# A vision tower whose first attention gets its input by batch: norm of batch 0 and mixed weights inside the embedding, both product layers by batch

## The reference, cut to what matters

```python
shifted = jnp.pad(x, ((0, 0), (1, 0), (0, 0)))[:, :-1]
delta = shifted - x
xr, xw, xk, xv, xa, xg = [x + delta * x_mix[i] for i in range(6)]
r = xr @ W_r
w = DECAY_SCALE * sigmoid(tanh(xw @ A_w) @ B_w + b_w)
k = xk @ W_k
v = xv @ W_v
a = sigmoid(xa @ A_a @ B_a + b_a)
g = sigmoid(xg @ A_g) @ B_g
```

## Time and profile before

| | us |
|---|---|
| median of 3 runs | 1413.83 (1410.52 to 1415.01) |
| the profiled execution | 1405.85 |
| its span | 1404.1 |
| TensorE busy, of the span | 1075.7 (77%) |
| VectorE | 905.2 (64%) |
| ScalarE | 763.8 (54%) |
| GpSimd | 166.3 (12%) |

### The profile page before, as it was taken

How to read it: one execution, slowest core, us unless ns; L and a number is a source line. 1 busy time by engine, 2 the same in 40 slices (tenths; PEclk the granted TensorE clock), 3 DMA queues, 4 the chain that set the end, 5 groups by cost and what they waited for, 6 DMA issues and landing times. The chain is left out here.

```text
span 1404.1 us, 27705 instructions
## 1 busy us (share of the span) xinstructions
PE 1075.7 (77%) x11369; PEld 609.2 (43%) x11369; DVE 905.2 (64%) x1932; ACT 763.8 (54%) x1071; POOL 166.3 (12%) x177
## 2 busy tenths in 40 slices
PE   5667974562879969935999999988799999997240
PEld 3456953351534444431333333354455556555220
DVE  0476547867891277775675555454799999984524
ACT  0452322221207643358999999932489898982020
POOL 0005402310002200000000000010024000000524
PEclk9788976765659979976999999978899999998575
DMA  7100000021000000000000000010000000002021
GB/s 148 29 1 1 4 4 17 0 35 43 3 1 1 1 0 1 1 2 3 1 2 1 1 1 1 2 29 14 1 2 2 2 3 3 2 2 68 13 46 27
DMA packets 42817, 18.23 MB, mean 13 GB/s; under 512 B 38069, under 2 KB 41641, under 8 KB 42437
## 3 DMA queue, kind: packets, MB, share of 16 engines
q1 hardware_dynamic: 40965, 15.39, 5.2%
q0 software_dynamic: 1728, 1.08, 0.4%
HBM read 12.95 MB, written 3.48 MB: 12 GB/s over the span
## 5 line engine op out<-in xcount | busy, mean ns | idle before, releaser
L2481 ACT ACTIVATE pt_PT<-ps 128x1024 f32<-128x1024 f32 x288 | 266.1, 1107 | 5.9 <-PE ps L2551 5.6
L3473 DVE TENSOR_SCALAR da_AD<-da_QH,da_XG,da_XH 128x1024 f32<-128x1024 f32 x296 | 231.3, 850 | 16.1 <-PE ps L3630 15.3
L3521 ACT ACTIVATE da_AD<-ps,da_NX 128x1024 f32<-128x1024 f32 x214 | 220.9, 1182 | 29.7 <-PE ps L3630 29.3
L3630 PE MATMUL ps<-da_AD,dw_win 128*32 128x256 f32 x4080 | 230.7, 382 | 4.6 <-DVE da_AD L3473 2.3
L3630 PEld LDWEIGHTS ps<-da_AD,dw_win 128*32 128x32 f32 x4080 | 130.2, 110 | 102.4 <-DVE da_AD L3473 15.1
L2517 PE MATMUL ps<-pt_PT,pa_V 128*32 128x512 f32 (+3 forms) x1536 | 155.5, 499 | 8.3 <-DVE pt_Yc L2458 3.2
L2465 DVE TENSOR_TENSOR pt_PT<-pt_PT,pt_keep 128x512 f32<-128x512 f32 x128 | 84.3, 689 | 61.2 <-ACT pt_PT L2481 60.1
L2551 PE MATMUL ps<-pt_QT,pt_KT 12*128 12x512 bf16 (+3 forms) x768 | 80.1, 334 | 3.2 <-DVE pt_KT L2423 0.5
L2517 PEld LDWEIGHTS ps<-pt_PT,pa_V 128*32 128x32 f32 x1536 | 38.9, 109 | 64.8 <-issue 63.6
L2090 ACT ACTIVATE mt_act<-ps 128x342 f32<-128x342 f32 (+1 forms) x66 | 30.1, 455 | 54.4 <-PE ps L2145 54.4
L2145 PE MATMUL ps<-mt_XF,ew_w 64*128 64x342 f32 (+1 forms) x132 | 54.6, 498 | 0.8 <-ACT mt_WT L2076 0.8
(11 more groups left out here) (789 smaller groups left out, 2053.0 us busy)
## 6 DMA issues: line engine op xcount, KB each, us to landing
em_xs<-in_x_dram SPq DMA_DIRECT2D x2, 1152.0 KB, 9.5
em_xs<-in_x_dram SPq DMA_DIRECT2D x2, 1024.0 KB, 13.8
cp_xbuf<-ci_zero SPq DMA_DIRECT2D x1, 672.0 KB
cp_XS<-cp_xbuf SPq DMA_DIRECT2D x8, 84.0 KB, 2.3
cp_ybuf<-cp_YS SPq DMA_DIRECT2D x8, 84.0 KB, 2.1
ew_win<-in_L_ffn_w_dram SPq DMA_DIRECT2D x2, 320.0 KB
em_WS<-in_L_tok_W_dram SPq DMA_DIRECT2D x8, 72.0 KB
la_blk<-la_scratch SPq DMA_DIRECT2D x8, 64.1 KB
```

Of the source, the lines that this page charges most:

```text
L2481: nc.scalar.activation(PT[:, n % RING, 2 * i:2 * i + 2, :], ps[:, b0:b0 + 2, :], ACT.Exp, scale=SCALE).then_inc(exp_ok, 1)
L3473: nc.vector.tensor_scalar(AD[:, j % RING], QH[:, b], XG[:, b, s:s + 1], XH[:, b, s:s + 1], ALU.max, ALU.subtract).then_inc(ad_dve, 1)
L3521: nc.scalar.activation(AD[:, j % RING], QA, ACT.Abs, bias=NX[:, b, s:s + 1]).then_inc(ad_act, 1)
L3630: ins = nc.tensor.matmul(o, D.win[:, int(by[j] == "D"), hp, 15 - m:47 - m], AD[:, j % RING, hp], start=False, stop=False, skip_group_check ...
```

## The change

The inputs of the projections get a class of their own, `ProjectionInputs` (R), made before the embedding; `stage_embed` is now called from `stage_rwkv`. In the embedding, SyncE also issues the 17 loads of weights and mix columns, behind all others; GpSimd fills BB and a corner of S and waits for the last three loads; VectorE mixes the weights after batch 0's copies, then computes batch 0's variance, and its norm after batch 1's copies; ScalarE takes batch 0's root between the third and the fourth copy to h; TensorE turns batch 0 in the middle of batch 1's products. The norm writes both halves of x2 itself (a broadcast over two), so GpSimd's copy is gone. In the projections TensorE transposes batch 0 and makes its first layer while VectorE norms batch 1; ScalarE copies both halves of S for batch 0, VectorE for batch 1. Transposes have banks 5, 6, 7, the first layer banks 0 to 5, and the second layer's banks are taken in an order in which it can wait by group.

```diff
+class ProjectionInputs:
...
+    def fill(self, nc, pool):
+        nc.gpsimd.memset(self.BB[:], 0.0).then_inc(self.nil, 1)
+        pool.wait_ge(self.nil, 1)
+        nc.gpsimd.memset(self.S[64:128, :, 0:1], 0.0).then_inc(self.nil, 1)
+        pool.wait_ge(self.nil, 2)
+        pool.wait_ge(self.b_in, 48)
+
+    def load(self, nc, sp, A):
+        for half in range(2):
+            rows = slice(64 * half, 64 * half + 64)
+            for _, name, c, n in self.ORDER:
+                sp.dma_start(self.WA[rows, c:c + n], A["L0_attn_" + name]).then_inc(self.w_in, 16)
...
+                sp.dma_start(self.mix[rows, :], A["L0_attn_x_mix"].rearrange("i d -> d i")).then_inc(self.mix_in, 16)
+        sp.wait_ge(self.nil, 1)
...
+    def mixed(self, nc, dve, link):
+        dve.wait_ge(self.mix_in, 32)
+        link(nc.vector.tensor_scalar(self.mix[0:64, :], self.mix[0:64, :], -1.0, 1.0, ALU.mult, ALU.add))
+        dve.wait_ge(self.w_in, 16 * self.LOADS)
+        for i, _, c, n in self.ORDER:
+            link(nc.vector.tensor_scalar(self.WA[:, c:c + n], self.WA[:, c:c + n], self.mix[:, i:i + 1], None,
+                                         ALU.mult))
+
+    def variance(self, nc, link, h, b, var_ready):
+        t = slice(NT * b, NT * b + NT)
+        x, st = self.xc[:, t], self.st
+        link(nc.vector.tensor_reduce(st[:, 0, t], h[:, t], AX.X, ALU.add))
+        link(nc.vector.tensor_scalar(st[:, 0, t], st[:, 0, t], 1.0 / 64, None, ALU.mult))
+        link(nc.vector.tensor_tensor(x, h[:, t], bcl(st[:, 0, t], 64), ALU.subtract))
+        link(nc.vector.tensor_tensor(self.tmp[:], x, x, ALU.mult))
+        link(nc.vector.tensor_reduce(st[:, 1, t], self.tmp[:], AX.X, ALU.add))
+        nc.vector.tensor_scalar(st[:, 1, t], st[:, 1, t], 1.0 / 64, 1e-5, ALU.mult, ALU.add).then_inc(var_ready, 1)
...
+    def normed(self, nc, dve, link, b, std_ready):
+        t = slice(NT * b, NT * b + NT)
+        dve.wait_ge(std_ready, 1)
+        link(nc.vector.reciprocal(self.st[:, 3, t], self.st[:, 2, t]))
+        twice = [P, NT, 2, 64]
+        return nc.vector.tensor_tensor(self.x2[:, t].rearrange("p t (i d) -> p t i d", i=2),
+                                       self.xc[:, t].unsqueeze(2).to_broadcast(twice),
+                                       self.st[:, 3, t].unsqueeze(2).unsqueeze(3).to_broadcast(twice), ALU.mult)
...
@@ stage_embed
+                R.load(nc, sp, A)
...
+                    if g == 2:
+                        R.root(nc, act, 0, var_ready, std_ready)
...
+                    if b == 0:
+                        R.mixed(nc, dve, link)
+                        dve.wait_ge(h_ok, 3)
+                        R.variance(nc, link, K.h, 0, var_ready)
+                    else:
+                        link(R.normed(nc, dve, link, 0, std_ready))
...
                     for l in range(16):
+                        if (b, l) == (1, 8):
+                            pe.wait_ge(emb_sb, 2)
+                            for g in range(3):
+                                turn(g)
...
-                pe.wait_ge(emb_sb, 2)
-                for g in range(3):
-                    turn(g)
...
@@ rwkv_projections
+        TURNS = (5, 6, 7, 6, 7, 6)
+        HIDS = (0, 2, 4, 0, 2, 4)
+        TBANK = (0, 1, 2, 3, 6, 7, 4, 5)
+        cols = lambda g, shift: slice((g % 3) * GRP + shift, (g % 3 + 1) * GRP + shift)
...
@@ vector
+                R.variance(nc, link, K.h, 1, var_ready)
+                R.normed(nc, dve, link, 1, std_ready).then_inc(x_ready, 1)
...
+                for g in range(3):
+                    hidden(g)
+                for g in range(3, NG):
                     dve.wait_ge(tr_ps, g + 1)
...
+                    nc.vector.tensor_copy(S[0:64, 1, cols(g, 0)], ps[0:64, TURNS[g], 0:GRP])
+                    nc.vector.tensor_copy(S[64:128, 1, cols(g, 1)], ps[64:128, TURNS[g], 0:GRP]).then_inc(s_dve, 1)
+                for g in range(3, NG):
+                    hidden(g)
...
@@ scalar
+                for g in range(3):
+                    act.wait_ge(tr_ps, g + 1)
+                    nc.scalar.copy(S[0:64, 0, cols(g, 0)], ps[0:64, TURNS[g], 0:GRP])
+                    nc.scalar.copy(S[64:128, 0, cols(g, 1)], ps[64:128, TURNS[g], 0:GRP]).then_inc(s_act, 1)
+                R.root(nc, act, 1, var_ready, std_ready)
...
@@ tensor
+                def hidden(g):
+                    pe.wait_ge(s_dve if g > 2 else s_act, g % 3 + 1)
+                    if g > 2:
+                        pe.wait_ge(hid_sb, g - 2)
+                        pe.wait_ge(sig_sb, 2 * (g - 2))
...
+                for g in range(3):
+                    turn(g)
+                for g in range(3):
+                    hidden(g)
                 pe.wait_ge(x_ready, 1)
...
-                pe.wait_ge(s_top, NG)
-                pe.wait_ge(s_bot, NG)
...
-                pe.wait_ge(hid_sb, NG)
-                pe.wait_ge(sig_sb, 2 * NG)
+                for g in range(3, NG):
+                    if g == 5:
+                        pe.wait_ge(s_dve, 1)
+                    turn(g)
+                for g in range(3, NG):
+                    hidden(g)
                 for t in range(T):
+                    if t < 8 and t % 2 == 0 and t != 4:
+                        done = {0: 4, 2: 5, 6: 6}[t]
+                        pe.wait_ge(hid_sb, done)
+                        pe.wait_ge(sig_sb, 2 * done)
```

More of the change, by code:

```diff
@@ L227, in stage_embed @@
         emb_ps, emb_sb, tr_ps, edge_ok = sem("emb_ps"), sem("emb_sb"), sem("tr_ps"), sem("edge_ok")
-        h_ok = sem("h_ok")
+        h_ok, chain, var_ready, std_ready = sem("h_ok"), sem("chain"), sem("var"), sem("std")
         ps = K.ps
@@ L246, in _ @@
                                  A["cls_tok"][0, 0, :].unsqueeze(1)).then_inc(cls_in, 16)
+                R.load(nc, sp, A)
+            @block.gpsimd
+            def _(pool):
+                R.fill(nc, pool)
             @block.scalar
@@ L324, in stage_rwkv @@
                    scaled_in=K.sem("rw_scaled_in"), chunks_in=K.sem("rw_chunks_in"))
-        rwkv_projections(nc, K, A, TM, pre)
+        with ExitStack() as front:
+            R = ProjectionInputs(K, front)
+            stage_embed(nc, K, A, R)
+            rwkv_projections(nc, K, A, TM, pre, R)
         QT = sb("QT", [128, T, 3, P])
@@ L365, in _ @@
             def _(sp):
[L366 to L375, removed]
                 for i, n in enumerate(("b_w", "b_a", "k_k", "k_a", "r_k")):
@@ L423, in _ @@
-                for g in range(NG):
-                    cols = slice(g * GRP, (g + 1) * GRP)
+                for g in range(3):
[3 more added lines that the diff above has]
+                R.root(nc, act, 1, var_ready, std_ready)
+                for g in range(NG):
+                    c = slice(g * GRP, (g + 1) * GRP)
@@ L439, in _ @@
-                pe.wait_ge(z_ok, 2)
-                pe.wait_ge(w_in, 240)
-                pe.wait_ge(s_top, NG)
-                pe.wait_ge(s_bot, NG)
-                for g in range(NG):
-                    if g >= 4:
-                        pe.wait_ge(hid_sb, g - 3)
-                        pe.wait_ge(sig_sb, 2 * g - 6)
-                    rhs = S[:, g // 3, (g % 3) * GRP:(g % 3 + 1) * GRP]
-                    nc.tensor.matmul(ps[:, (2 * g) % 8, 0:GRP], WA[:, 192:320], rhs,
-                                     start=True, stop=True).then_inc(hid_ps, 1)
-                    nc.tensor.matmul(ps[:, (2 * g + 1) % 8, 0:GRP], WA[:, 320:448], rhs,
-                                     start=True, stop=True).then_inc(hid_ps, 1)
@@ L452, in _, with turn, hidden @@
-                pe.wait_ge(hid_sb, NG)
-                pe.wait_ge(sig_sb, 2 * NG)
+                def turn(g):
+                    for j in range(3):
+                        ins = nc.tensor.transpose(ps[:, TURNS[g], j * P:(j + 1) * P], x2[:, 3 * g + j, :],
+                                                  K.ident[0:P, 0:P])
+                    ins.then_inc(tr_ps, 1)
+                def hidden(g):
+                    pe.wait_ge(s_dve if g > 2 else s_act, g % 3 + 1)
+                    if g > 2:
+                        pe.wait_ge(hid_sb, g - 2)
+                        pe.wait_ge(sig_sb, 2 * (g - 2))
+                    rhs = S[:, g // 3, cols(g, 0)]
+                    nc.tensor.matmul(ps[:, HIDS[g], 0:GRP], WA[:, 192:320], rhs,
+                                     start=True, stop=True).then_inc(hid_ps, 1)
+                    nc.tensor.matmul(ps[:, HIDS[g] + 1, 0:GRP], WA[:, 320:448], rhs,
+                                     start=True, stop=True).then_inc(hid_ps, 1)
```

90 lines of the change are left out of this document (36 added, 54 removed).

## The result

The changed kernel took 1397.53 us (median of 4 runs, 1391.25 to 1403.48), the kernel before beside it 1414.42 (4 runs): ratio 0.9895, 95% interval 0.9859 to 0.9931. It is faster by about 1%, as forecast; the number lies 4.9 us under the forecast and 1.0 under its range. More runs put both in their place. All 93 timed runs of the kernel before have the mean 1410.7; the median that the forecast started from lay 3.1 above it. Sixteen of the changed kernel have 1397.9 (a seventeenth, at 1654.67, is left out: its mean granted clock was 0.617, that of the others 0.843 to 0.856). The gain is 12.8 us, against 11.4 forecast; in the two later sets of runs with both kernels side by side it is 12.7 and 11.5. That the two are so close is in part chance: the front (all that lies before the third block) gave less than forecast, 8.3 us, and something that the front does not show gave the rest.

A forecast was written before the change was run, and what follows sets the result against it. A chain passing between engines, mostly one working at a time from 42.00 to 67.40, bounds the front. Losing 1.9 us in the embedding and winning 13.3 in the projections gives 1413.8 - 11.4 = 1402.4 us, range 1398.5 to 1408.5.

The forecast's parts named there:

- 8.4 us to batch 1's first layer: Projections: from the second block's start at 43.9 to batch 1's first layer at 52.3.
- the upper bound, 1.36: Projections, batch 1's norm: the multiply writing 1152 elements from 576 lies between 0.75 and 1.36 us; 1.36 was taken.
- TensorE starts batch 1 at 30.50: Embedding: batch 1's products start at 30.50, as in the kernel before, and need 7.10 us.
- as forecast (1.9): Embedding: the second block begins at 43.9 in place of 42.00, a loss of 1.9 us.
- No idle stretch is longer than 1.8 us, so I take the products at full clock: New front: TensorE idles at most 1.8 us (39.5 to 41.3), so its products run at granted clock 1.00.
- The rival of the low clock: Batch 1's first layer runs at low clock, costing 1.5 us: gain 9.9, time 1403.9; chance 0.14.
- Rows 11: Profile rows cited for TensorE's clock staying at 1.00 over 2 us in which it worked 0.57.
- The 17 end at 19.6 at 0.6 each: Embedding: SyncE issues weights and mix columns from 9.4, 0.6 us each, ending at 19.6.
- both rivals of late weights: Embedding: issues stall until 30.5, delaying VectorE's mixing: 1408.2 us, chance 0.08; with slow issues too, 1417.8, chance 0.04.
- The cover: Embedding: the mixing ends by 34.3 while VectorE is wanted at 36.4, leaving 2.1 us spare.
- The rival of a dearer switch: Projections, ScalarE: a table switch takes twice its 1.28 us load: gain 9.8, time 1404.0; chance 0.02.
- nothing lasting: Later blocks: the earlier start shifts TensorE's clock falls, 1.5 us each; three leave 6.9 of gain, 1411 us; chance 0.06.

The follow-up runs named there:

- the run above: The changed kernel with SyncE waiting until x of batch 1 has landed before it issues the 17 weight loads; 1408.47 us, ratio 0.9984.
- all late: The changed kernel with seven linked zero fills on VectorE that SyncE waits for before the first load; 1410.53 us, ratio 0.9999.
- only the third block late: The changed kernel with six linked zero fills on VectorE behind its last copy into TM, ending the second block; 1408.46 us, ratio 0.9979.
- the shorter chain: The changed kernel with class tokens moved, one PSUM copy on ScalarE, H1 copies between those into S, first sigmoid before tanh; 1397.93 us, ratio 0.9917.

## Why the prediction was right, and where it was wrong

**The mechanism** was right. The second block starts with three engines at work, and from its start to the second layer it takes 13.5 us in place of 25.4. The forecast's 8.4 us to batch 1's first layer came out at 8.41; the multiply took the upper bound, 1.36; the variance 3.45 of 3.6.

**"TensorE starts batch 1 at 30.50"** failed: 31.83, and 32.00 and 32.57 in the other two traces (30.79 in the second of before). It is 1.3 of the 3.4 us by which the second block comes later; from there on the embedding cost 2.0, as forecast (1.9). The first folded product starts at 9.6 to 10.4 in the eleven traces with the new embedding that started on time, and at 8.90 and 9.53 in the kernel before. The weights in the queue are not the cause (9.75 without them). What it is stays open, and with two traces of before so does how large it is.

**"No idle stretch is longer than 1.8 us, so I take the products at full clock"** is the step that was wrong. No idle stretch was longer, and the clock fell all the same, in every trace of this order: the low clock covered batch 1's layer in two, batch 0's in the others. The rival of the low clock, given 0.14, is what happened; its price of 1.5 was right for batch 1's layer (5.05 - 3.48 = 1.57). The price hangs on the place: from the second block's start to the second layer the changed kernel takes 13.46 and 13.43 us with the late fall and 12.66 with the early one, and 11.79 when everything starts late and the clock is back by 58.5. Rows 11 showed a clock that held over 2 us; they said nothing of a longer stretch of turns and waits. And the fall in the kernel before was read as coming after idle time alone, 2.1 us of it from 41.90; ahead of it TensorE had made only turns, from 37.52, and in the second trace of that kernel the clock fell at 42.7, about 1.1 us after the last turn. The Trainium skill (TensorE: Matmul & The Clock Gate, Part 4: PE-mode transpose) says that transposes do not count towards the clock as products do. The late falls, at 53.5 and 53.4, come behind turns that are such transposes and agree with it. The early ones come behind the embedding's turns, which the kernel writes as ordinary products with an identity, and say nothing for it. And in the kernel before the clock rises in a stretch in which TensorE makes only such transposes (from 105.00 to 107.00 the windows give 0.89, after 0.50), which the statement does not cover.

**"The 17 end at 19.6 at 0.6 each"** was wrong: there was a stall, of the kind on which both rivals of late weights rested. The cover held, since the stall ended by 24.8, before x had landed, and not at 30.5 as that rival had it. Of the 2.1 us of cover 1.6 are left. Had the issues begun only with x landed, the run above shows what it costs: 5.5 us.

**The table loads**: each 1.28, and the sigmoid follows 0.02 later. The rival of a dearer switch is out. The Trainium skill (ScalarE: Activation LUTs, What ACT_TABLE_LOAD costs) adds about 1380 ns of drain to a switch; this trace does not show it.

**What the front does not show.** The means differ by 12.8 us, the starts of the third block by 8.8 (82.5 and 73.7, means of two and three traces). From that start to the end the traces have:

| kernel | third block | rest of the span |
|---|---|---|
| before, two traces | 81.92, 83.16 | 1322.2, 1326.6 |
| changed, three | 73.66, 73.79, 73.79 | 1328.1, 1329.7, 1317.7 |
| all late | 81.25 | 1320.1 |
| only the third block late | 81.01 | 1327.2 |

The rest scatters by 12 us with the same instructions and the same start, and its mean is no shorter for the changed kernel (1325.2 against 1324.4). So these traces can't show where 4 us went. The timed runs of the late kernels, 11.8 and 10.2 above the changed one for 7.5 and 7.3 of start, suggest that part of it goes with the time at which the later stages start. The clearest comparison is within one chip: the shorter chain and the all-late kernel start the third block 8.1 us apart (73.16 and 81.25) and their means lie 11.7 apart (1398.0 and 1409.8), with an uncertainty of 1.3. The forecast's "nothing lasting" had this the wrong way round: the shift did not eat the gain but came with more.

The first 21 us of the third block are not where it happens: VectorE's operations there start at the same distance from the block's start, within 0.03 us, in all seven traces of the table. TensorE's clock is the likeliest place. Within one kernel the time of a run falls by 0.8 to 1.0 us for every 0.001 by which its mean granted clock is higher, and that mean is 0.849 for the changed kernel, 0.844 and 0.842 for the two late ones and 0.842 before. Part of these differences is idle time at half clock in the front itself, which costs nothing, so they do not prove it. No stage was found that does it, and it stays open.

## What to carry to other kernels

When a block is a chain through all engines, split it by batch: of the front's gain that gave some 5 us (by difference), and moving the weights and one norm into the block before gave 2 each. Work moved onto an engine's list delays what stands behind it, so price it by the next thing on that engine's list. Where bursts of TensorE alternate with waits, take the low clock for the likeliest case, even with waits under 2 us; a microsecond saved elsewhere may move the fall, and its price changes with its place.

## What was not expected of the hardware

- TensorE's clock fell to 0.50 with idle stretches of at most 1.67 us in the 12 us ahead of the fall (at 53.5, in the first trace of the changed kernel). Where it fell changed from one execution to the next of one program (worked out from the windows' means: at 53.5, 53.4 and 45.1 in three traces of the changed kernel), and with it the price: the early fall cost 0.8 us less than the late ones, counted from the second block's start to the second layer.
- One DMA issue held SyncE's queue for 10.3 to 10.9 us in nine traces, the eighth of the 17 loads, with the embedding's own loads in flight; in two edited kernels the same time was spread over two and three issues from that one on. The same 17 loads, issued once x had landed, took 0.47 to 0.65 each.
- Of one program, the 1320 us behind the front took from 1317.7 to 1329.7 in three traces. A change of a few us in a stage is read in that stage's timeline, not in the span of one execution.
